# Attention weights times values: the values streamed from rows of a token's columns, laid out by ScalarE

## The reference, cut to what matters

```python
q = (x @ wq.T + bq).reshape(B, S, 32, 16)      # k, v alike
scores = einsum('bshd,bstd->bsht', q, k) / 4   # 32 x 32 for each token
probs = softmax(scores, axis=-1)
context = einsum('bsht,bstd->bshd', probs, v).reshape(B, S, 512)
x = layernorm(x + context)
h = silu(x @ dq(w1).T) * (x @ dq(w2).T)        # hidden 1376, dq: NF4 quantise and dequantise, blocks of 64
x = layernorm(x + h @ dq(w3).T)
```

## Time and profile before

| what | value |
|---|---|
| three timed runs | 785.93, 788.27, 789.87 us; median 788.27 |
| the profiled execution | 788.01 us, of which the span of the trace is 786.2 us |
| mean granted TensorE clock | 0.862 of full speed |
| PE / PEld / DVE / ACT / POOL busy | 93 / 80 / 81 / 62 / 14% of the span |
| instructions | 14305 |

### The profile page before, as it was taken

How to read it: one execution, slowest core, us unless ns; L and a number is a source line. 1 busy time by engine, 2 the same in 40 slices (tenths; PEclk the granted TensorE clock), 3 DMA queues, 4 the chain that set the end, 5 groups by cost and what they waited for, 6 DMA issues and landing times.

```text
span 786.2 us, 14305 instructions
## 1 busy us (share of the span) xinstructions
PE 732.7 (93%) x5688; PEld 625.5 (80%) x5688; DVE 633.4 (81%) x876; ACT 484.6 (62%) x650; POOL 106.8 (14%) x101
## 2 busy tenths in 40 slices
PE   4899999966999989999999999999999999999983
PEld 4778788856999989999888877887887788888761
DVE  2699999975888988988888899999977986554386
ACT  3588979773645636546853878877756775333134
POOL 2011012113101101111101121121201111000022
PEclk9999999995555655555799999999999999999995
DMA  9964455999797695995413371211514010330347
GB/s 219 223 182 146 134 166 167 250 305 271 166 261 189 184 283 134 269 216 202 163 26 122 120 230 54 81 39 31 173 59 155 1 61 21 134 119 13 121 147 160
DMA packets 89474, 117.89 MB, mean 150 GB/s; under 512 B 24768, under 2 KB 70848, under 8 KB 86496
## 3 DMA queue, kind: packets, MB, share of 16 engines
q1 hardware_dynamic: 88272, 114.88, 51.6%
q10 hardware_dynamic: 1136, 2.10, 1.2%
HBM read 76.42 MB, written 38.86 MB: 147 GB/s over the span
## 4 chain that ended last, share of the span: by engine, by line
PE 54%; DVE 18%; issue 11%; ACT 8%; DMA 4%; SPq 4%; POOL 1%; DVEq 0%; POOLq 0%; ACTq 0%
PE ps_p L1043 10%; DVE nf_acc L1166 8%; PE ps_s L947 7%; PE ps_s L945 7%; PE ps_s L946 7%; PE ps_p L945 5%; PE ps_p L947 5%; PE ps_p L946 5%; ACT nf_y L777 4%; PE ps_s L1030 3%; PE ps_t L968 2%; DMA qk_parts<-qk_p 2%; DVE part L1298 2%; DMA k_st<-qk_parts 1%; ACT part L852 1%
## 5 line engine op out<-in xcount | busy, mean ns | idle before, releaser
L1166 DVE SCALAR_TENSOR_TENSOR nf_acc<-nf_y,nf_acc 128x1024 f32<-128x1024 f32 (+4 forms) x266 | 298.5, 1122 | 37.6 <-ACT nf_y L777 28.3
L777 ACT ACTIVATE nf_y<-nf_w,bound_b 128x1024 f32<-128x1024 f32 (+4 forms) x285 | 288.9, 1047 | 9.7 <-DVE nf_acc L1162 3.4
L1043 PE MATMUL ps_p<-probT,v_bd 128*68 128x32 f32 x1024 | 125.7, 301 | 7.9 <-issue 7.9
L1043 PEld LDWEIGHTS ps_p<-probT,v_bd 128*68 128x68 f32 x1024 | 122.7, 211 | 9.4 <-issue 8.0
L945 PE MATMUL ps_p<-x_hl,w_hl 128*128 128x512 f32 x192 | 77.6, 404 | 6.1 <-DVE w_hl L1184 4.1
L695 POOL TENSOR_TENSOR nf_w<-nf_w,nf_rec 128x1024 f32<-128x1024 f32 (+4 forms) x19 | 39.5, 2080 | 320.1 <-DVE nf_rec L1150 320.1
L1325 DVE TENSOR_TENSOR silu<-silu,ps_s 128x512 f32<-128x512 f32 (+1 forms) x44 | 30.1, 684 | 61.5 <-PE ps_s L947 61.5
L927 ACT ACTIVATE hid_hl<-silu 128x512 fp32r<-128x512 f32 (+1 forms) x44 | 27.8, 632 | 77.6 <-DVE silu L1325 77.6
L947 PE MATMUL ps_p<-x_hl,w_hl 128*128 128x512 f32 x192 | 75.5, 393 | 0.0
L945 PE MATMUL ps_s<-x_hl,f_ha 128*128 128x512 f32 x192 | 75.4, 393 | 0.0
L946 PE MATMUL ps_p<-x_hl,w_hl 128*128 128x512 f32 x192 | 75.3, 392 | 0.0
(11 more groups left out here) (110 smaller groups left out, 1253.1 us busy)
## 6 DMA issues: line engine op xcount, KB each, us to landing
x_hl<-x_parts SPq DMA_DIRECT2D x10, 2048.0 KB, 8.5
qk_parts<-qk_p SPq DMA_DIRECT2D x64, 204.0 KB, 2.6
q_st<-qk_parts SPq DMA_DIRECT2D x48, 272.0 KB, 6.8
k_st<-qk_parts SPq DMA_DIRECT2D x48, 272.0 KB, 7.2
x_parts<-x_st SPq DMA_DIRECT2D x16, 512.0 KB, 4.4
nf_w<-in_L_ffn_w SPq DMA_DIRECT2D x24, 256.0 KB, 3.0
dequantised<-nf_acc SPq DMA_DIRECT2D x10, 512.0 KB, 2.6
v_blocks<-v_t SPq DMA_DIRECT2D x16, 256.0 KB, 3.5
```

The costliest lines, as they stand in the source:

```text
L777: act.activation(nf_y[0:p, at % NY, 0:w], nf_w[0:p, u % 2, 0:w], ACT.Identity, bias=bound_b[0:p, i:i + 1], scale=STEEP).then_inc(s_ny, 1)
L1043: t = pe.matmul(ps_p[0:MV, (G + 3) % NPV, i * H:(i + 1) * H], v_bd[hb % 2][:, :, g * GI + i], probT[:, G % 2, i], start=True, stop=True)
L1166: dve.scalar_tensor_tensor(out=acc, in0=y, scalar=float(NF4[i + 1]), in1=acc, op0=ALU.min, op1=ALU.max).then_inc(s_nacc, 1)
```

## The change

*Values.* The tile `v_bd` becomes [128, 64, 68]: for one column i, the 68 entries lie side by side. The matmul's sides are swapped: the weights are `probT` of one i (32 columns) and `v_bd[:, i]` streams (68 columns). The four i of a group of four go to four column groups (partitions 32j of the PSUM bank), and the result of a round is [128, 4 x 68] with heads along the partitions. As the later steps want heads along the columns, ACT copies it out (`evacuate`, to `ctmp`, three buffers), PE transposes it back in four transposes (`back`), and ACT copies that to `ctx` as before (`context`).

*Laying out.* SP loads values into one new tile `v_c` [128, 16, 64] in the order of before, and ACT writes them into `v_bd` with 16 side by side (`put_values`, one q of a half-block at a time): all four of half-block 0 in round 0 after `exp(0)`, and of half-block hb one in each of rounds 4hb-2 to 4hb+1, after `exp` and `evacuate`. `load_v(hb+1)` waits for the four of hb (`s_vput`).

*Places.* `values(G-2)` now stands ahead of the ct turns; `back(G-3)` behind them; `context(G-4)` replaces `context(G-3)`. ct turns, moments, `norm_1` and xt turns are one round later (the last xt pair in the tail), and so are the rounds with one level step. ACT takes its first half of level steps ahead of `context`.

*First loads.* `load_v(0)` is issued at tau = 47, ahead of the last store; the queries of half-block 1 come after it and are no longer between the stores.

*Also:* `pairs(g)` in place of fixed pairs of weight columns in the feed-forward's turns (the last, narrow one alone); an unused tile of 3008 bytes a partition is put among the feed-forward's tiles.

```diff
@@ -93,10 +93,19 @@
+    def pairs(g):
+        js, out = list(GROUPS[g]), []
+        while js:
+            n = 2 if len(js) > 1 and rows_of(js[1]) == P else 1
+            out.append(js[:n])
+            js = js[n:]
+        return out
...
         kind, g, _ = UNITS[u]
-        return [("f", u, s) for s in range(2 if kind == "w" else -(-len(GROUPS[g]) // 2))]
+        return [("f", u, s) for s in range(2 if kind == "w" else len(pairs(g)))]
@@ -132,15 +141,15 @@
-    FIRST_STACKS = {FIRST_LOAD + at: which for at, which in ((0, (0, 0)), (2, (0, 1)), (4, (0, 2)),
-                                                             (6, (1, 0)), (7, (1, 1)), (8, (1, 2)))}
+    FIRST_STACKS = {FIRST_LOAD: 0, FIRST_LOAD + 2: 1, FIRST_LOAD + 4: 2}
     VALUES_FREE = 3 * KC * NBK - KC
+    FIRST_VALUES = 3 * KC * NBK - 1
...
     for b in range(NBK - 1):
-        LV_A[8 * b + 10:8 * b + 13] = [1, 1, 1]
+        LV_A[8 * b + 11:8 * b + 14] = [1, 1, 1]
@@ -161,20 +170,22 @@
     HEADS = [range(0, 7), range(7, 14), range(14, 21), range(21, 28), range(28, 32)]
-    CT_AT, XT_AT, MOMENTS_AT, NORM_AT, F_AT = {}, {}, {}, {}, {}
+    CT_AT, XT_AT, MOMENTS_AT, NORM_AT = {}, {}, {}, {}
...
         for k in range(len(HEADS)):
-            CT_AT.setdefault(8 * b + 10 + k // 2, []).append(("ct", b, k))
-        MOMENTS_AT[8 * b + 12] = b
-        NORM_AT[8 * b + 13] = b
+            CT_AT.setdefault(8 * b + 11 + k // 2, []).append(("ct", b, k))
+        MOMENTS_AT[8 * b + 13] = b
+        NORM_AT[8 * b + 14] = b
         for c in range(KC):
-            XT_AT.setdefault(8 * b + 14 + c // 2, []).append(("xt", b, c))
-    LATE = {8 * b + 8 + k: 8 * b + 13 for b in range(NBK - 1) for k in range(2)}
-    CONTEXT_AT = {}
+            XT_AT.setdefault(8 * b + 15 + c // 2, []).append(("xt", b, c))
+    BACK_AT, CONTEXT_AT = {}, {}
+    LATE = {8 * b + 8 + k: 8 * b + 14 + k // 2 for b in range(NBK - 1) for k in range(4)}
     for G in range(GG):
-        CONTEXT_AT.setdefault(max(G + 3, LATE.get(G, 0)), []).append(G)
-    for G in range(GG):
+        CONTEXT_AT.setdefault(max(G + 4, LATE.get(G, 0)), []).append(G)
+        BACK_AT.setdefault(G + 4 if G % 8 == 2 and G > 8 else G + 3, []).append(G)
+    for G in range(GG + 1):
@@ -276,15 +287,17 @@
         q_st1 = sb("q_st1", [P, H, TS], BF16, att)
-        v_bd_0 = sb("v_bd_0", [P, MV, TI], F32, att)
+        v_c = sb("v_c", [P, D, TI], F32, att)
+        v_bd_0 = sb("v_bd_0", [P, TI, MV], F32, att)
...
         ctx = sb("ctx", [MV, H, P], F32, att)
-        v_bd_1 = sb("v_bd_1", [P, MV, TI], F32, att)
+        v_bd_1 = sb("v_bd_1", [P, TI, MV], F32, att)
         x1_st = sb("x1_st", [P, 2, 2, BK], F32R, att)
+        ctmp = sb("ctmp", [P, NCT, 4 * MV], F32, att)
@@ -541,15 +559,21 @@
                 for q in range(Q4):
-                    sp.dma_start(v_bd[hb % 2][32 * q:32 * q + 32, DV * q:DV * q + D],
+                    sp.dma_start(v_c[32 * q:32 * q + 32],
                                  v_d[hb].rearrange("(d t) s -> t d s", d=D)[:, :, TI * q:TI * q + TI]
-                                 ).then_inc(s_ldv[hb % 2], 16)
+                                 ).then_inc(s_ldv, 16)
+            def store_x1(key):
+                _, b, c = key
+                low_done(sp, key)
+                sp.dma_start(x1_d[b, :, :, c], x1_st[:, c % 2].bitcast(F32)).then_inc(s_stx[c % 2], 16)
...
                     sp.wait_ge(s_pv, GG - NG)
+                    sp.wait_ge(s_vput, Q4 * NHB)
@@ -604,11 +628,12 @@
                 if tau in FIRST_STACKS:
-                    hb, b = FIRST_STACKS[tau]
-                    load_stacks(sp, hb, [b], range(2) if hb == 0 else [0])
-            values_stored(sp, KC)
-            sp.wait_ge(s_vzero[0], 2 * Q4)
-            load_v(0)
+                    load_stacks(sp, 0, [FIRST_STACKS[tau]])
+                if tau == FIRST_VALUES:
+                    values_stored(sp, KC)
+                    sp.wait_ge(s_proj, VALUES_FREE)
+                    load_v(0)
+            load_stacks(sp, 1, sides=[0])
@@ -618,10 +643,7 @@
                 if g == 1 and hb + 1 < NHB:
-                    if hb:
-                        sp.wait_ge(s_pv, NG * hb)
-                    else:
-                        sp.wait_ge(s_vzero[1], 2 * Q4)
+                    sp.wait_ge(s_vput, Q4 * (hb + 1))
@@ -723,13 +743,13 @@
                 for q in range(Q4):
-                    pool.memset(v_bd[slot][:, DV * q:DV * q + DV], 0.0).then_inc(s_vzero[slot], 1)
+                    pool.memset(v_bd[slot][:, GI * q:GI * q + GI], 0.0).then_inc(s_vzero[slot], 1)
...
                 for q in range(Q4):
-                    pool.memset(v_bd[slot][32 * q:32 * q + 32, DV * q + D], 1.0).then_inc(s_vzero[slot], 1)
+                    pool.memset(v_bd[slot][32 * q:32 * q + 32, :, DV * q + D], 1.0).then_inc(s_vzero[slot], 1)
@@ -834,15 +854,33 @@
+            def put_values(hb, q):
+                if q == 0:
+                    act.wait_ge(s_ldv, 16 * Q4 * (hb + 1))
+                    if hb < 2:
+                        act.wait_ge(s_vzero[hb], 2 * Q4)
+                    else:
+                        act.wait_ge(s_pv, NG * (hb - 1))
+                act.activation(v_bd[hb % 2][32 * q:32 * q + 32, :, DV * q:DV * q + D],
+                               v_c[32 * q:32 * q + 32].rearrange("p d i -> p i d"), ACT.Copy).then_inc(s_vput, 1)
+            def evacuate(G):
+                if G == 0:
+                    values_stored(act, KC * NBK)
+                act.wait_ge(s_pv, G + 1)
+                wait(act, s_back, G - NCT + 1)
+                act.activation(ctmp[:, G % NCT], ps_p[:, G % 2, 0:4 * MV], ACT.Copy).then_inc(s_evac, 1)
...
                 b, e = divmod(hb, 2)
-                act.wait_ge(s_pv, G + 1)
+                act.wait_ge(s_back, G + 1)
...
                 act.activation(ctx[:, :, at:at + GI],
-                               ps_p[0:MV, (G + 3) % NPV].rearrange("p (i h) -> p h i", h=H), ACT.Copy
+                               ps_p[0:MV, 2 + G % 2].rearrange("p (i h) -> p h i", h=H), ACT.Copy
@@ -887,10 +925,18 @@
             for G in range(GG):
+                steep(LV_A[G] // 2)
...
                     context(at)
-                steep(LV_A[G] // 2)
                 exp(G)
+                if G >= 2:
+                    evacuate(G - 2)
+                if G == 0:
+                    for q in range(Q4):
+                        put_values(0, q)
+                hb, g = divmod(G + 2, NG)
+                if 0 < hb < NHB:
+                    put_values(hb, g)
@@ -901,16 +947,17 @@
                 steep(LV_A[G] - LV_A[G] // 2)
+            context(GG - 4)
+            evacuate(GG - 2)
+            for key in XT_AT.get(GG, []) + TAIL_1:
+                high(key)
             context(GG - 3)
-            for key in TAIL_1:
-                high(key)
-            context(GG - 2)
...
                 high(key)
-            context(GG - 1)
+            evacuate(GG - 1)
+            context(GG - 2)
             steep(LV_T[1])
@@ -920,6 +967,8 @@
                 act.activation(silu[0:rows, s % 2], ps_s[0:rows, 0], ACT.Silu).then_inc(s_silu, 1)
+                if s == 0:
+                    context(GG - 1)
@@ -1036,13 +1085,24 @@
                 if g == 0:
-                    pe.wait_ge(s_ldv[hb % 2], 16 * Q4 * (hb // 2 + 1))
+                    pe.wait_ge(s_vput, Q4 * (hb + 1))
                 pe.wait_ge(s_probT, G + 1)
-                wait(pe, s_ctx, G - NPV + 1)
+                wait(pe, s_evac, G - 1)
                 for i in range(GI):
-                    t = pe.matmul(ps_p[0:MV, (G + 3) % NPV, i * H:(i + 1) * H], v_bd[hb % 2][:, :, g * GI + i],
-                                  probT[:, G % 2, i], start=True, stop=True)
+                    a, j = divmod(i, 4)
+                    t = pe.matmul(ps_p[32 * j:32 * j + 32, G % 2, a * MV:(a + 1) * MV], probT[:, G % 2, i],
+                                  v_bd[hb % 2][:, g * GI + i], start=True, stop=True)
                 t.then_inc(s_pv, 1)
+            def back(G):
+                pe.wait_ge(s_evac, G + 1)
+                wait(pe, s_ctx, G - 1)
+                for a in range(4):
+                    t = pe.transpose(ps_p[0:MV, 2 + G % 2, P * a:P * a + P], ctmp[:, G % NCT, a * MV:(a + 1) * MV],
+                                     ident[:])
+                t.then_inc(s_back, 1)
@@ -1102,22 +1162,28 @@
                 scores(G)
+                if G >= 2:
+                    values(G - 2)
...
                     turn(key)
-                if G >= 2:
-                    values(G - 2)
+                for at in BACK_AT.get(G, []):
+                    back(at)
...
             values(GG - 2)
-            for key in TAIL_1:
+            for key in XT_AT.get(GG, []) + TAIL_1:
                 turn(key)
+            back(GG - 3)
...
                 turn(key)
+            back(GG - 2)
...
                 gate_up(s)
+                if s == 0:
+                    back(GG - 1)
```

(24 more changed lines are left out.)

4 lines of the change are left out of this document (1 added, 3 removed).

## The result

| | median | lowest to highest | runs |
|---|---|---|---|
| before | 787.10 us | 785.30 to 789.87 | 4 |
| after | 856.69 us | 855.32 to 858.60 | 4 |

The ratio is 1.0885 (95%: 1.0861 to 1.0909). The profiled execution took 856.5 us with a span of 854.7, so +68.5 us where +32.6 was forecast. The mean granted TensorE clock is 0.861, as before (0.862).

A forecast was written before the change was run, and what follows sets the result against it. Bound: attention's closed loop over vector and scalar engines, 4.88 us a round, tensor engine within 0.3 us. Sum: 788.0 + 20.0 (rounds and tail) + 10.6 (start) + 2 (later value loads) = 820.6, say 821 us; range 800 to 847.

The forecast's parts named there:

- spreading 0.96 us: Scalar engine's copy of values into v_bd, between exponential and second level step: 0.96 us each, upper bound twice that.
- rival 2: Strided spreading costs double: another 0.96 us in 23 spreadings, 0.8 us in nine context rounds, 849 us; chance 0.12.
- later value loads: Waits for later half-blocks' values through the one staging tile: six times 0 to 5 us, taken as +2 us.
- start: Start of the attention stage: scalar engine waits in order for first values; +10.6 us, from 0 to +14.
- tail: End of attention: one pair of output transposes slips in, +2.0 us, and the last way back, +0.5 us.
- context rounds: Attention rounds where vector engine's 3.1 us of context adding hides 2.9 us of scalar engine work: -4.4 us.
- The bound and the loop: Attention's closed scalar and vector engine loop, 4.88 us, takes evacuation and spreading unhidden: plain round 6.2 us.
- Rival 1: Scalar engine's 86 us of waiting takes the 47 us of new work, hiding it all: 775 us; chance 0.11.
- Evacuation: Scalar engine's copy of 272 elements a round, after the exponential: 0.44 us, 0.33 with overlap in the loop.
- Values matmuls: Tensor engine's values matmuls with sides swapped: 2.1 us a round instead of 3.96, bounds 0.7 to 4.2 us.
- ways back: Tensor engine's four transposes a round returning the values' result, 0.24 us each: 1.0 us a round.
- Rival 3: Swapping the values matmuls' sides gains nothing: values at 4.2 us, tensor round 6.5 us plain, 844 us; chance 0.10.

The follow-up runs named there:

- e9: Kernel before, with the 68 weight columns of each values matmul side by side, loaded values left out; 787.69 us, one run.
- e5: Kernel after, each spreading reading its 1024 elements in a row and writing runs of 16, values landing in wrong places; 838.84 us, ratio 1.0665.
- e2: Kernel after, each spreading writing only one of its 64 columns, with waits, loads and places kept; 827.31 us, ratio 1.0523.
- e3: Kernel after, spreading of rounds 2 to 29 moved behind the round's second level step; 828.16 us, ratio 1.0525.
- e12: Kernel after with quarter loads, evacuation behind the second level step, and spreading done by GpSimd instead of the scalar engine; 817.31 us, ratio 1.0390.
- e6: Kernel after, value loads issued quarter by quarter, each right after the spreading that frees its part; 850.46 us, ratio 1.0816.
- e4: Kernel before, with only the change's new order of first loads; 787.93 against 787.03 us, ratio 1.0016.
- e8: Kernel after, all four values matmuls of a group sent to one column group, results overwriting each other; 855.49 us, one run.
- e10: Kernel after, spreading of rounds 2 to 29 behind the second level step and value loads quarter by quarter; 825.62 us, ratio 1.0499.
- e11: Kernel after, quarter loads, with both evacuation and spreading behind the second level step; 827.71 us, ratio 1.0523.
- e1: Kernel after, spreading reading 64 neighbouring floats in a row and writing with a 272-byte step; 859.36 us, ratio 1.0924.

## Why the prediction was wrong

The direction was right, the time (821 us, range 800 to 847) was too low by 36 us. The step that failed is the term "spreading 0.96 us", taken at its lower bound because the context copy with its strided PSUM read cost no more than the exponential. That row is of another memory; the nearest case with a step in SBUF was the strided weight load, which I had named as the reason for the upper bound. It was a weak witness too: by e9 its step takes a round from 2.16 to 3.96 us near the full clock, but only from 3.84 to 3.96 at 0.50. What happened is rival 2, to which I gave a chance of 0.12. Its 849 us are still 8 short: later value loads 4.2, start 2.7, tail 0.9.

The spreading does not carry the whole miss by itself. With it at 1.10 us the kernel takes 839 (e5), so its size is worth 17.9 of the 36 us. Of the rest 10 us are later loads (11.9 us of waits in e5 where I had 2), and 6 lie in the context rounds and the rounds with output transposes, which grew by more than I forecast even then; why, the runs do not say.

The range was too narrow by its own terms: start from 0 to +14 and six loads of 0 to 5 us reach from 808 to 852, not 804 to 834. And the range of 800 to 847 was said to take in most of rival 2, whose own time of 849 lies outside it.

- *The bound and the loop: right.* The chain of after is the chain of the earlier trace rows with the two new links in it. e2 shows the slope (1.91 us less spreading, 1.90 us less of a plain round), e3 that the place is what counts (28.5 us), e12 the old 4.88 us with both links out. Rival 1, that the scalar engine's idle time would take the work, is refuted by the same runs: the idle time ahead of the exponential went only from 86.4 to 67.5 us.
- *The spreading's size: wrong.* 2.04 us, of which e5 gives 0.94 to the step. 28 spreadings in the rounds at 1.08 us more make 30.2 us, worked out; e5 measured 17.9 us for 32 of them at 0.94 less each, with 9.6 us of new load waits against it. In it is the miss of 9.6 us in the context rounds: the vector engine's 3.1 us of contexts were to hide 2.9 us on the scalar engine, which became 4.0.
- *Evacuation: right.* 0.383 us, overlapping by nothing that the chain shows (forecast 0.33 in the loop).
- *Later value loads: mis-sized.* +6.2 us instead of +2; e6 took 8.9 us off the waits and 6.2 off the time. Four of the six later loads came in time, as the forecast's slack says; the other two were late by 3.3 and 2.9 us. In e5, with shorter rounds, three were late, by 6.1, 2.2 and 3.6 us.
- *Start: nearly right.* +13.3 against +10.6. The load times came as forecast (177, 197 against 176.6, 198.7); the four spreadings took 7.86 us. That the reordered loads gain nothing was right (e4, 1.0016).
- *Values matmuls: mis-sized, of no account.* 1.13 us a round, not 2.1; ways back 1.07 for 1.0. The tensor round is 3.55 us instead of 4.4, off the path either way (e8). Rival 3 is refuted.
- *Tail:* +3.4 from the last transposes to the feed-forward, forecast +2.5.

The sum: 30.2 (spreading) + 4.2 (later loads) + 2.7 (start) + 0.9 (tail) = 38.0 us for a miss of 35.9 in the profiled run. One of the 2 us too many is the spreading of round 2, which is in the 30.2 and again in the start. The normalising rounds 14 and 22 also grew by 2.0 and 1.1 us only, where evacuation and spreading came to 2.5; the four rounds with output transposes grew by 2.5 to 2.8 us each, so there they were paid in full.

What stays open: whether any place for the spreading wins. In the places tried on the scalar engine it doesn't (e3, e10, e11: its sum bounds the plain rounds at 5.3 to 5.9 us); on GpSimd the old loop comes back, and 30 us remain over before, in copies of 2.6 us, lifts stretched beside them and queue waits, which I did not separate. A second staging tile, and stores or loads issued from another queue, were not tried; e10 and e12, in which such waits are left, suggest them. No version here beat the kernel before.

## What to carry to other kernels

Before pricing new work on an engine with idle time, find whether the idle time lies in the same arc of the closed loop as the new work: here 67 to 86 us of idle time stood ahead of the exponential and the work went in behind it, so every microsecond of it counted in every plain round. A copy that steps through SBUF on either side is priced by a row that steps through SBUF, not by one that reads PSUM; with no such row, a value at the lower bound needs a reason, and here the upper bound was right. And a wait that one change removes comes back where the next load or buffer was about to be late: the order of first loads moved a wait by one round, and quarter loads with the late spreading moved it from values to stores.

## What the runs showed that I had not expected

- A scalar-engine copy of 32x1024 float32 takes 1.10 us with the read in a row and the write in runs of 16, 2.04 us with a 256-byte step in the read, 2.10 us with a 272-byte step in the write (after, e1, e5).
- The float32 matmuls with 32 weight columns and 68 streamed take 3.83 us for 16 (32 records) on one column group and 1.13 us on four, both at the clock 0.50 (e8, after).
- 68 weight columns at a step of 256 bytes: 3.96 us a round at the clock 0.50 and at 0.93; side by side 3.84 at 0.50 and 2.16 at 1.00 (before, e9).
- The spreading copy takes 2.62 us on GpSimd, and a lift of the vector engine beside it took up to 3.24 us for 1.29; which of them holds the other up was not measured (e12).
